# An RWKV-and-feed-forward block on one core: a new written-out order, work moved between engines, and the variance of four sequences in two fp32r passes

## What is computed

```
xn = (x - mean) / sqrt(var + 1e-5)                      # per row
shifted = xn moved down one row in its sequence
k, v, r = (xn*m + shifted*(1-m)) @ W,  one m and W each
per channel, along the sequence (a scan of num, den, mx):
    out = (e1*num + e2*v) / (e1*den + e2)
s = (sigmoid(r) * out) @ Wo
h = relu(xn @ w1 + b1);  z = xn + h @ w2 + b2           # expert 0 alone: the routing weights are set to it
g = silu(layernorm(z)*gamma + beta)
result = x + s*g
```

## Time and profile before

| | |
|---|---|
| median of 3 runs | 112.2 us (111.92 to 112.39) |
| profiled execution, first to last instruction | 110.7 us |
| busy: TensorE, VectorE, ScalarE, GpSimd | 101.9, 96.0, 94.3, 66.0 us |
| granted TensorE clock, mean | 0.996 |
| moved by DMA | 5.09 MB |

### The profile page before, as it was taken

The page is one execution under the profiler, slowest core; times in us unless marked ns, Lnnn a source line. Parts: engine busy times, 40 slices in busy tenths (PEclk is TensorE's granted clock), DMA queues, the critical chain, the costliest instruction groups (busy, mean ns, idle before and its releaser), DMA issues. The chain is left out here.

```text
span 110.7 us, 1604 instructions
## 1 busy us (share of the span) xinstructions
PE 101.9 (92%) x336; PEld 56.7 (51%) x336; DVE 96.0 (87%) x199; ACT 94.3 (85%) x155; POOL 66.0 (60%) x104
## 2 busy tenths in 40 slices
PE   4997799997999999999999999999999999999660
PEld 4993335553465445553675553674554566435230
DVE  1647989979999999799988989999999897899980
ACT  1425087899999998999899999999999999999940
POOL 3009998986746469459999998743819403360000
PEclk9999999999999999999999999999999999999998
DMA  3999200000000000000002110000000002203134
GB/s 98 284 314 288 61 3 0 0 6 0 0 3 3 0 0 0 0 0 0 0 0 95 46 57 0 0 0 0 3 0 0 3 0 95 81 14 95 46 101 143
DMA packets 9450, 5.09 MB, mean 46 GB/s; under 512 B 481, under 2 KB 9185, under 8 KB 9441
## 3 DMA queue, kind: packets, MB, share of 16 engines
q1 hardware_dynamic: 8880, 4.59, 14.7%
q10 hardware_dynamic: 560, 0.40, 1.3%
HBM read 2.89 MB, written 2.10 MB: 45 GB/s over the span
## 5 line engine op out<-in xcount | busy, mean ns | idle before, releaser
L638 PE MATMUL bank<-hid,w_c 128*128 128x512 f32 x64 | 31.1, 592 | 0.0
L589 PE MATMUL bank<-mixed,w_in 128*128 128x512 f32 x48 | 24.1, 599 | 0.8 <-POOL mixed L379 0.7
L475 ACT ACTIVATE hid<-bank,vec 128x512 f32<-128x512 f32 x32 | 21.4, 683 | 1.1 <-PE bank L611 0.7
L716 DVE SCALAR_TENSOR_TENSOR mixed<-step_x,vec,bank 128x511 f32<-128x511 f32 x24 | 17.5, 738 | 1.6 <-POOL step_x L370 1.6
L638 PEld LDWEIGHTS bank<-hid,w_c 128*128 128x128 f32 x64 | 11.9, 190 | 10.8 <-issue 9.3
L609 PE MATMUL bank<-xT_hi,w_hi 128*128 128x512 f32 x28 | 15.5, 552 | 1.1 <-POOL xT_lo L361 1.1
L589 PEld LDWEIGHTS bank<-mixed,w_in 128*128 128x128 f32 x48 | 8.4, 189 | 10.1 <-issue 8.6
L370 POOL TENSOR_TENSOR step_x<-xT 128x512 f32<-128x512 f32 x8 | 8.3, 1037 | 8.5 <-ACT xT L467 8.4
L403 POOL TENSOR_TENSOR dv<-v_sb 128x512 f32<-128x512 f32 x8 | 9.8, 1227 | 5.8 <-ACT v_sb L526 5.8
L340 POOL TENSOR_SCALAR xn<-x_sb,neg_mean,rstd 128x128 f32<-128x128 f32 x28 | 12.2, 449 | 0.0
L755 DVE TENSOR_TENSOR_SCAN dev<-keep,dv 128x512 f32<-128x512 f32 x8 | 9.8, 1220 | 1.7 <-issue 0.8
(11 more groups left out here) (70 smaller groups left out, 201.3 us busy)
## 6 DMA issues: line engine op xcount, KB each, us to landing
x_sb<-x SPq DMA_DIRECT2D x7, 256.0 KB, 6.6
block_out<-res SPq DMA_DIRECT2D x7, 256.0 KB, 2.3
w_in<-squares SPq DMA_DIRECT2D x1, 256.0 KB, 3.0
w_in<-w ACTq DMA_DIRECT2D x1, 256.0 KB, 5.4
w_in<-w SPq DMA_DIRECT2D x1, 256.0 KB, 6.3
block_out<-res SPq DMA_DIRECT2D x2, 128.0 KB, 1.9
x_sb<-x SPq DMA_DIRECT2D x1, 128.0 KB, 2.2
x_sb<-x ACTq DMA_DIRECT2D x1, 128.0 KB, 2.6
```

The costliest lines, as they stand in the source:

```text
L475: act.activation(hid[b % 2][:, f, :], ps(f"up{f}", b)[:, :], ACT.Relu, bias=vec[:, B1_COLUMN + f:B1_COLUMN + f + 1]).then_inc(done[f"hid{f ...
L589: pe.matmul(ps(name, b)[:, :], w_in[:, which, :], mixed[b % 2][:, which, :], start=True, stop=True).then_inc(done[name], 1)
L638: pe.matmul(ps("z", b)[:, :], w2_c[:, f, :], hid[b % 2][:, f, :], start=False, stop=chunks_of(b)[-1] == f"z{f}", skip_group_check=True).th ...
L716: dve.scalar_tensor_tensor(mixed[n][:, which, 1:], step_x[n][:, 1:], vec[:, which:which + 1], ps("z", b)[:, 0:T - 1], ALU.mult, ALU.add).t ...
```

## The change

The four engine lists and the banks are written anew, with the sequences staggered in another way. Beside the order:

- **Other engines for steps.** `hid1:1 hid1:3 hid3:3 hid1:5 hid2:6 hid0:6 hid3:7` go from ScalarE to VectorE; `rel` of all sequences but 2 from VectorE to GpSimd; `d:0` from GpSimd to VectorE; `xT_hi:1` from GpSimd to ScalarE. Semaphores are now counted per engine and step.
- **Results moved from PSUM to SBUF.** e_new, ln_den and th_a have SBUF tiles of their own. The bank of k comes free after gap.
- **Variance.** For sequences 3 to 6 GpSimd rounds the squares to fp32r (`sq_hi`) and subtracts that from them (`sq_lo`), and TensorE averages both, in two fp32r matmuls onto one bank, with an fp32r copy of the averaging matrix.
- **Start.** The first sequence goes in halves through bn, aggr1, ve, rs, norm1, T, xT and the up-projections. `WARM_UP` 11 becomes 7, `KEEP_WARM` 4 becomes 2. w1 is loaded second on SyncE's queue, ahead of the squares (before: third on ScalarE's), and the second sequence third on ScalarE's (before: third on SyncE's).
- **End.** The last result's second half is stored from ScalarE's queue; its halves go b before a.

```diff
-WARM_UP = 11
-KEEP_WARM = 4
+WARM_UP = 7
+KEEP_WARM = 2
...
     "dve": """
+        bn.a:0 aggr1.a:0 bn.b:0 aggr1.b:0 norm1.a:0 norm1.b:0 cols bn:1 aggr1:1 d:0 w2_sum ink:0
+        inr:0 inv:0 bn:3 mx:0 bn:2 gap:0 aggr1:2 aggr1:3 bn:6 bn:7 bn:5 den:0 ink:1 hid1:1 inv:1
+        inr:1 mx:1 ink:2 gap:1 aggr1:7 aggr1:5 bn:4 mx:2 aggr1:4 aggr1:6 gap:2 zn:0 inr:2 inv:2
+        dev:0 den:1 ink:3 adev:0 den:2 wkv:0 zn:1 hid1:3 rel:2 gated:0 hid3:3 inr:3 dev:1 inv:3
+        adev:1 mx:3 wkv:1 gap:3 dev:2 gated:1 adev:2 wkv:2 prod:0 gated:2 ink:4 den:3 inv:4 inr:4
+        mx:4 ink:5 gap:4 zn:2 inv:5 zn:3 mx:5 gap:5 dev:3 hid1:5 adev:3 res:0 prod:1 wkv:3 inr:5
+        gated:3 den:4 den:5 ink:6 inv:6 prod:2 zn:4 mx:6 hid2:6 gap:6 inr:6 dev:4 ink:7 adev:4 inr:7
+        wkv:4 gated:4 hid0:6 mx:7 gap:7 inv:7 den:6 zn:5 res:1 res:2 den:7 dev:5 hid3:7 adev:5
+        prod:3 wkv:5 prod:4 zn:6 gated:5 dev:6 adev:6 dev:7 wkv:6 adev:7 gated:6 wkv:7 res:3 gated:7
+        prod:5 res:4 prod:6 zn.b:7 zn.a:7 res:6 prod.b:7 prod.a:7 res:5 res.b:7 res.a:7
     """,
     "pool": """
+        w1_lo nm:1 fix:0 norm1:1 w2_c d:1 xT_lo:1 gmax:0 gmin:0 nm:2 fix:1 norm1:2 dv:0 rel:0 d:2
+        xT_hi:2 fix:2 xT_lo:2 gmin:1 norm1:3 gmax:1 keep:0 gmax:2 gmin:2 xT_hi:3 d:3 xT_lo:3 nm:4
+        norm1:4 rel:1 dv:1 keep:1 fix:3 norm1:5 dv:2 keep:2 xT_hi:4 d:4 xT_lo:4 gmin:3 fix:4 gmax:3
+        sq_hi:3 sq_lo:3 norm1:6 d:5 rel:3 fix:5 xT_hi:5 xT_lo:5 keep:3 dv:3 gmin:4 gmax:4 gmin:5
+        gmax:5 norm1:7 sq_hi:4 sq_lo:4 d:6 xT_hi:6 fix:6 xT_lo:6 rel:4 dv:4 keep:4 rel:5 d:7 gmin:6
+        gmax:6 sq_hi:5 fix:7 sq_lo:5 keep:5 xT_hi:7 xT_lo:7 gmin:7 gmax:7 dv:5 sq_hi:6 sq_lo:6 rel:6
+        dv:6 rel:7 keep:6 dv:7 keep:7
     """,
...
-FREED_BY = {"z": ["zn"], "k": ["adev"], "v": ["v_sb", "wkv"], "r": ["gated"], "up0": ["hid0"], "up1": ["hid1"],
+FREED_BY = {"z": ["zn"], "k": ["gap"], "v": ["v_sb", "wkv"], "r": ["gated"], "up0": ["hid0"], "up1": ["hid1"],
...
             load_half(sp, 0)
+            sp.dma_start(w1_in[:, :], w1).then_inc(got["w1"], 16)
             sp.dma_start(w_in[:, :, :], squares).then_inc(got["squares"], 16)
-            load(sp, 1)
...
+            pool.tensor_copy(averager_r[:, :], averager[:, :]).then_inc(prep["averager_r"], 1)
...
+            def square_high(b):
+                after(pool, "sq", b)
+                after(pool, "var", b - 2)
+                pool.tensor_copy(sq_hi[b % 2][:, :], sq[b % 2][:, :]).then_inc(done["pool", "sq_hi"], 1)
+
+            def square_low(b):
+                after(pool, "sq_hi", b)
+                after(pool, "var", b - 2)
+                pool.tensor_tensor(sq_lo[b % 2][:, :], sq[b % 2][:, :], sq_hi[b % 2][:, :].bitcast(FP32),
+                                   ALU.subtract).then_inc(done["pool", "sq_lo"], 1)
...
-                act.activation(ps("k", b)[:, :], gap_min[b % 2][:, :], ACT.Exp, bias=neg_td[:, :]).then_inc(done["e_new"], 1)
+                act.activation(e_new[b % 2][:, :], gap_min[b % 2][:, :], ACT.Exp,
+                               bias=neg_td[:, :]).then_inc(done["act", "e_new"], 1)
...
+                if ("sq_hi", "", b) in signal:
+                    once(pe, b, "averager_r", 1, first_on("pool", "sq_hi"))
+                    after(pe, "sq_hi", b)
+                    after(pe, "sq_lo", b)
+                    pe.matmul(ps("var", b)[:, :], averager_r[:, :], sq_hi[b % 2][:, :], start=True, stop=False)
+                    pe.matmul(ps("var", b)[:, :], averager_r[:, :], sq_lo[b % 2][:, :], start=False,
+                              stop=True).then_inc(done["pe", "var"], 1)
+                    return
...
-                dve.tensor_tensor_scan(den[n][:, 1:], e_keep[n][:, :], ps("k", b)[:, :], 1.0,
-                                       ALU.mult, ALU.add).then_inc(done["den"], 1)
+                dve.tensor_tensor_scan(den[n][:, 1:], e_keep[n][:, :], e_new[n][:, :], 1.0,
+                                       ALU.mult, ALU.add).then_inc(done["dve", "den"], 1)
...
-                dve.scalar_tensor_tensor(adev[n][:, :], ps("k", b)[:, :], 1.0, dev[n][:, :],
-                                         ALU.add, ALU.mult).then_inc(done["adev"], 1)
+                dve.scalar_tensor_tensor(adev[n][:, :], th_a[n][:, :], 1.0, dev[n][:, :],
+                                         ALU.add, ALU.mult).then_inc(done["dve", "adev"], 1)
```

More of the change, by code:

```diff
@@ L53 @@
[L53 to L57, removed]
@@ L100, in tokens, with signal_table @@
         yield named(token)
+def signal_table():
+    count, table = {}, {}
+    for engine in PROGRAM:
+        for name, half, b in tokens(engine):
+            count[engine, name] = count.get((engine, name), 0) + 1
+            table[name, half, b] = (engine, count[engine, name])
+    return table
 def bank_tables():
@@ L207, in build_block @@
         prep = {n: sem(f"prep_{n}") for n in
-                ["ident0", "ident", "consts", "edges", "neg_td", "cols", "b2_mean", "w1_hi", "w1_lo", "wo",
+                ["ident0", "ident", "consts", "edges", "neg_td", "cols", "b2_mean", "w1_hi", "w1_lo", "wo", "averager_r",
                  "w2_sum", "w2_mean", "w2"]}
-        STEPS = (["bn", "aggr1", "ve", "rs", "nm", "norm1", "T", "xT", "xT_hi", "xT_lo",
-                  "d", "fix", "ink", "inv", "inr", "k", "v", "r", "v_sb",
-                  "mx", "gap", "gmin", "gmax", "e_new", "e_keep", "den", "ln_den", "rel",
-                  "th_g", "th_a", "keep", "dv", "dev", "adev", "wkv", "th_r", "gated", "s"]
-                 + [f"up{f}" for f in range(NF)] + [f"hid{f}" for f in range(NF)]
-                 + [f"z{f}" for f in range(NF)] + ["sq", "var", "ln_var", "rstd2", "zn", "silu", "prod", "back", "res"])
-        done = {n: sem(f"done_{n}") for n in STEPS}
+        done = {(engine, name): sem(f"{name}_by_{engine}")
+                for engine, name in dict.fromkeys((signal[token][0], token[0]) for token in signal if token[2] is not None)}
         stored = [sem(f"stored_{n}") for n in range(2)]
@@ L290, in load, with store @@
                           x_rows[b]).then_inc(got[f"x{b}"], 16)
+        def store(eng, b, half=""):
+            after(eng, "res", b, half)
+            eng.dma_start(out_rows[b][:, tiles(half), :], res[b % 2][:, tiles(half), :]).then_inc(stored[b % 2], 16)
         block = ctx.enter_context(nc.Block())
@@ L301, in _ @@
                 load(sp, b)
-            for b in range(B):
-                for half in ("a", "b") if b == LAST and "res" in HALVED else ("",):
-                    after(sp, "res", b, half)
-                    sp.dma_start(out_rows[b][:, tiles(half), :], res[b % 2][:, tiles(half), :]).then_inc(stored[b % 2], 16)
+            for b in range(LAST):
+                store(sp, b)
+            store(sp, LAST, "a")
             sp.wait_ge(stored[0], 16 * (B // 2))
-            sp.wait_ge(stored[1], 16 * (B // 2 + ("res" in HALVED)))
+            sp.wait_ge(stored[1], 16 * (B // 2 + 1))
         @block.gpsimd
@@ new lines, in low_part, with value_steps @@
+            def low_part(b):
+                n = b % 2
+                after(dve, "xT_hi", b)
+                for f in range(NF):
+                    after(dve, f"up{f}", b - 2)
+                dve.tensor_tensor(xT_lo[n][:, :], xT[n][:, 1:], xT_hi[n][:, :].bitcast(FP32),
+                                  ALU.subtract).then_inc(done["dve", "xT_lo"], 1)
+            def value_steps(b):
+                n = b % 2
+                once(dve, b, "edges", EDGES, first_on("dve", "dv"))
+                after(dve, "v_sb", b)
+                after(dve, "dev", b - 2)
+                dve.tensor_tensor(dv[n][:, :], v_sb[n][:, 1:], v_sb[n][:, 0:T],
+                                  ALU.subtract).then_inc(done["dve", "dv"], 1)
@@ L812, in _ @@
             steps.update({"in" + name: mix(name) for name in "kvr"})
+            steps.update({f"hid{f}": hidden(f) for f in range(NF)})
             run("dve", steps)
```

362 lines of the change are left out of this document (199 added, 163 removed).

## The result

The changed kernel takes **123.0 us** (median of 4 runs, 122.62 to 123.13), the kernel before 112.2 beside it: a ratio of 1.095, 95% interval 1.092 to 1.098. It is 9.5% slower: 8.4 us above the forecast of 114.6, 6.5 above the range of the likeliest case (112.8 to 116.5) and 5 above the 118 up to which the rivals reached.

A forecast was written before the change was run, and what follows sets the result against it. It took TensorE and ScalarE to bound the middle, VectorE close behind. From 112.2 us, VectorE's gains of 2.8 and its remaining collision cost of 5.2 gave +2.4, so 114.6 us, with a range of 112.8 to 116.5.

The forecast's parts named there:

- the likeliest case: The forecast itself: VectorE's collisions with GpSimd outweigh its gains, 112.8 to 116.5 us, chance 0.38.
- the rivals: Collisions hide (109.4 us, chance 0.36), GpSimd becomes the bound (117.6, 0.14), gain and price cancel (112.2, 0.12).
- By itself that is hidden: GpSimd's added work, from 66.0 to 79.2 us, fits in some 95 us between its first split and the end.
- 4 x 0.39 = 1.6 us less: TensorE: variance of sequences 3 to 6 as two fp32r passes, 0.47 us for 0.86 each.
- the netting of the collisions: VectorE: of 8.8 us of waits for GpSimd, 3 us of middle idle time hide some, 5.2 stay.
- Both sides are one queue, so they aren't added: Collisions: VectorE's sum, +2.4 us, and GpSimd's, -0.7 to +3.3, are alternatives; +2.4 is taken.
- What the new order is worth: VectorE before collisions: 1.5 us gained at the start, 0.7 added, 2.0 of middle idle time back: -2.8 us.
- That VectorE is held up: VectorE's two-SBUF-input den, dev and adev wait for running GpSimd instructions: 4.8 + 4 = 8.8 us.
- Its sign of 8 us or more of idle time in the middle: A sign that the forecast is right: VectorE idle for 8 us or more in the middle.
- GpSimd as the bound: Rival, chance 0.14: GpSimd's late keeps delay the next gaps; decides if the last keep comes after 98; 117.6 us.
- The tail: From GpSimd's last keep to the last result, VectorE's operations and gaps take 10.6 us.
- The start: First transpose near 5.2 us instead of 6.37; VectorE dense from 7.6 to 20 us, 1.5 us gained.

The follow-up runs named there:

- e10: The changed kernel with dev and adev reading a PSUM bank (other values), no split of the squares and four result buffers: 110.3 us.
- e11: The changed kernel without the split of the squares and with four result buffers, collisions left in: 117.4 us.
- e6: The changed kernel with the old warm-up (WARM_UP 11, KEEP_WARM 4): 122.1 us.
- e4: The changed kernel without the split of the squares, the variance of sequences 3 to 6 again one fp32 matmul: 119.2 us.
- e5: The changed kernel with four result buffers instead of two: 120.9 us.
- e9: The kernel before with dev reading v's PSUM bank in place of dv (other values): 111.9 us.
- e2: The kernel before with e_new, ln_den and th_a in SBUF tiles, same order: 120.8 us.
- e3: The changed kernel with dev and adev reading v's PSUM bank in place of dv and th_a (other values): 114.9 us.
- e1: A separate kernel: VectorE runs one instruction beside eight GpSimd instructions; a scan with two SBUF inputs takes 1.54 or 2.21 us for 1.22 alone.
- e8: The kernel before with the squares of sequences 3 to 6 split by GpSimd, var and ln_var one to four places later: 118.4 us.
- e7: The kernel before with e_new alone moved to SBUF: 116.3 us.

## Why the prediction was wrong, step by step

**The miss in three parts.** The forecast was 114.6, the time 123.0. By e10 and e11 the 8.4 us between them are 5.6 for the split and the result buffers, which the sum had at no cost; 1.9 for the collisions of dev and adev (7.1 us for the 5.2 left after netting, den's not counted in the 7.1); and 0.9 for everything else (110.3 for 109.4), den's collisions among it. About 1 us of the 5.6 may be the slow first up-projections (e6).

**The steps that failed.** The first is "By itself that is hidden", said of GpSimd's added work, with the split entered only as "4 x 0.39 = 1.6 us less" on TensorE. The split costs 2.4 us with two result buffers (e4, less its head start) and 3.8 with four (e5 to e11). The sum left out the latency, sq to var to ln_var, on three lists issued in order, and the later last keep (5.1 us earlier without the split, 1.7 of it the head start). In the one place shown TensorE waited 2.09 us for sq_lo, more than the 1.6 us that all four averages were to save.

The second is the netting of the collisions ("the 3 us of idle time left in the middle hide some"): 8.8 less 5.2 hides 3.6 us, more than the 3 that it names. From e11 to e10 VectorE's lengthening falls by 7.7 us and the time by 7.1, while VectorE's idle time from 20 to 103 us was 3.4 without these collisions and 2.0 with them. So little was netted on VectorE, which was nearly full; on GpSimd in the old order, a third of it idle, the 2.8 us by which dev alone held it up were hidden whole (e9). The likely reason for VectorE, not tested by itself, is that VectorE's pauses are waits on others that come again after each delay.

"Both sides are one queue, so they aren't added" does not hold in the old order, where e2 costs 9.1 us, more than either side's lengthening (5.6 and 8.4), though less than both together. In the new order it comes out: 7.1 us is not the sum of 7.7 and 10, but near VectorE's side.

The third step is a term that the sum didn't have, the wait of a result for the store that frees its buffer: 3.5 us at the end of the changed kernel, 2.2 in the time (e5).

**What the new order is worth: right in kind, 1.6 for 2.8.** Without the collisions of dev and adev, the split and the result buffers' waits the new order runs in 110.3 us, 1.4% under the old one rid of its collisions (e9, 111.9). The forecast had 109.4, with the split's gain in it, so the two are not quite like for like. The moves of rel to GpSimd and of the seven activations to VectorE were not tried one by one in the new order.

**That VectorE is held up: right.** 8.8 us were estimated for its side, and its rows are longer by 8.6. Its sign of 8 us or more of idle time in the middle did not come (5.1 of 83 us, 5.9 before): a held-up instruction counts as busy. On GpSimd's side 11.0 were estimated and 16.1 are there; besides, rel alone takes 1.27, not step_x's 1.04 (7 x 0.23 = 1.6), which the row of xT_lo in the earlier trace rows, also with two different tiles, would have given.

**GpSimd as the bound**, given 0.14, is what the profile shows from 20 to 103 us, and the last keep came at 104.4, past the 98 from which it was to decide. The case's own time, 117.6, fell short by the tail (14.0 for 10.6), by 1.4 us of the keep, and by 0.5 of what follows the last result. It is a part of the cause: taking 8.5 us of work from it brings the last keep 3.4 us earlier, the head start taken off (e4), while taking the collisions of dev and adev away gives 8.1 in the time (e3). Of its 94.4 us 16.1 are held-up time.

**The tail** of 10.6 is right in e5, e10 and e11 (10.5 to 10.6). The tail was made of VectorE's lengths and gaps alone, without the waits for stores.

**The start**: the first transpose comes at 5.35 (5.2 said), but the up-projections in halves took 5.17 us in this execution, so k:0 starts at 12.29 against 11.18 before. The 1.5 us of VectorE's start did not come here: between 8 and 20 us it is busy for 10.97 us, before for 10.91. With the faster first pieces it is 11.97 in e4 and e10, so about 1 us of the gain was to be had.

What den's eight collisions cost within the 110.3 was not tried in the new order; their rows are longer by 0.7 us in e10.

No version with the right values was found that is faster than the kernel before. To have e10's time, dev and adev would need an input each in PSUM, where `BANKS` has holders for all eight banks; no such layout was tried.

## What to carry to other kernels

Before a tile is moved from PSUM to SBUF, ask which VectorE instructions then read two SBUF inputs, and charge each its wait for GpSimd's running instruction (half of one was near enough here, 8.8 us for 8.6), look for the delay of what GpSimd makes next, and set little idle time against it: VectorE, busy for 93% of the middle, took up 1.4 of 7.7 us. In lists issued in order between bounded engines, a cheaper operation that comes through another engine is paid in latency and in the time that its bank stays held: look at who has the bank next, not only at who needs the product. And when an order brings results closer together, count their buffers and the stores that free them.

## What was not expected of the hardware

VectorE and GpSimd share by whole instructions and in e1 by turns: one GpSimd instruction between four scans waited for one (1.28 us for 0.62). Yet one scan of the new order lost two turns in a row to GpSimd (3.77 us for 1.22), at the same place in four traces, so turns can't be counted on. TensorE's granted clock fell to its lower level for 1.7 us and more behind a wait of 2.09 us in the changed kernel, and matmuls there took up to twice their time; it fell behind one of 1.87 us in e8 too, but not behind waits of 1.82 us in the changed kernel and 2.03 in e7. And the first half-width matmuls took 5.17 us in one execution and 3.70 in five others, with the granted clock at 1.00 in both that were looked at.
